# Twenty instead of eight shared groups ahead of the experts, with all late sends among them

## What is computed

```python
h = table[x]                                   # embedding
h = h + attention(layernorm(h))                # 8 heads
x2 = layernorm(h)
shared = gelu(x2 @ Ws1 + bs1) @ Ws2 + bs2      # for every row, 128 -> 512 -> 128
y = shared + bank(x2, sp) + bank(x2, fq)       # two banks of 8 experts each
out = h + y
# bank: each row goes to its top-1 expert, which takes 1280 rows at most;
#       expert = gelu(rows @ W1 + b1) @ W2 + b2, times the gate
```

## Time and profile before

| | |
|---|---|
| median of 3 runs | 1516.28 us (1511.69 to 1517.81) |
| span of the profiled execution | 1551.0 us (the page gives this and no other time of it) |
| PE busy | 1486.1 us, 96% of the span |
| DVE, ACT, POOL busy | 1049.6, 1148.1, 969.7 us |
| mean granted TensorE clock | 0.990 |

### The profile page before, as it was taken

The page is one execution under the profiler, slowest core; times in us unless marked ns, Lnnn a source line. Parts: engine busy times, 40 slices in busy tenths (PEclk is TensorE's granted clock), DMA queues, the critical chain, the costliest instruction groups (busy, mean ns, idle before and its releaser), DMA issues. The chain is left out here.

```text
span 1551.0 us, 33789 instructions
## 1 busy us (share of the span) xinstructions
PE 1486.1 (96%) x11128; PEld 1370.1 (88%) x11128; DVE 1049.6 (68%) x2810; ACT 1148.1 (74%) x3470; POOL 969.7 (63%) x998
## 2 busy tenths in 40 slices
PE   6789999999999999999999999978889999999999
PEld 3479999999999999999999999877888999999999
DVE  7977787788788788778788787642333343346666
ACT  6788888888888888888888888844444555556655
POOL 7575568887887887887887886643566566520000
PEclk9999999999999999999999999989999999999999
DMA  7224412112111111111111110112333323456665
GB/s 261 114 74 160 145 40 68 48 48 59 38 40 58 37 35 56 34 34 48 43 34 37 54 34 26 58 45 56 75 94 83 85 72 87 120 153 190 184 191 146
DMA packets 171503, 126.48 MB, mean 82 GB/s; under 512 B 30309, under 2 KB 154959, under 8 KB 171330
## 3 DMA queue, kind: packets, MB, share of 16 engines
q1 hardware_dynamic: 153794, 104.15, 22.7%
q0 software_dynamic: 17536, 20.17, 4.7%
HBM read 61.64 MB, written 78.66 MB: 90 GB/s over the span
## 5 line engine op out<-in xcount | busy, mean ns | idle before, releaser
L1138 ACT ACTIVATE expd<-masked,nmax 128x128 f32<-128x128 f32 x1024 | 395.9, 393 | 0.2 <-DVE nmax L1286 0.2
L938 POOL TENSOR_TENSOR prob<-expd,rtotal 128x1024 f32<-128x1024 f32 x128 | 243.2, 1900 | 126.8 <-DVE rtotal L1255 121.3
L1275 DVE COPY_PREDICATED masked<-off_diag,ps_s 128x1024 f32<-128x1024 int32 x128 | 174.7, 1365 | 143.5 <-PE ps_s L1031 143.5
L1071 PE MATMUL ps_o<-u,probT 128*128 128x128 f32 x2048 | 249.1, 275 | 0.0
L1071 PEld LDWEIGHTS ps_o<-u,probT 128*128 128x128 f32 x2048 | 239.0, 191 | 0.0
L1138 ACT ACTIVATION_READ_ACCUMULATOR expd<-masked,nmax 128x1 f32 x1024 | 196.6, 192 | 0.0
L1147 ACT ACTIVATE u<-ps_ut 128x1024 f32<-128x1024 f32 x128 | 131.4, 1026 | 66.5 <-PE ps_ut L1082 55.2
L1162 ACT ACTIVATE probT<-ps_ut 128x1024 f32<-128x1024 f32 x128 | 131.5, 1027 | 45.5 <-PE ps_ut L1039 37.9
L1231 DVE TENSOR_TENSOR w_lo<-ps_w,w_hi 128x512 fp32r<-128x512 f32 x256 | 164.4, 681 | 0.9 <-ACT w_hi L1171 0.9
L1171 ACT ACTIVATE w_hi<-ps_w 128x512 fp32r<-128x512 f32 x256 | 146.2, 596 | 15.9 <-PE ps_w L1057 9.3
L1286 DVE TENSOR_REDUCE nmax<-masked 128x8 f32<-128x1024 f32 x128 | 155.6, 1216 | 2.4
(11 more groups left out here) (252 smaller groups left out, 3914.8 us busy)
## 6 DMA issues: line engine op xcount, KB each, us to landing
turned<-x2T SPq DMA_DIRECT2D x32, 256.0 KB
answers_sp<-zeros SPq DMA_DIRECT2D x16, 512.0 KB
answers_fq<-zeros SPq DMA_DIRECT2D x16, 512.0 KB
xT<-turned SPq DMA_DIRECT2D x56, 128.0 KB
sh_back<-answers_sp SPq DMA_DIRECT2D x56, 128.0 KB, 2.3
sh_back<-answers_fq SPq DMA_DIRECT2D x56, 128.0 KB, 2.5
out<-res SPq DMA_DIRECT2D x56, 128.0 KB, 2.1
h_sb<-in_L_tok_weight SPq DMA_DIRECT2D x12, 512.0 KB, 6.2
```

The lines of the kernel that those rows point to most:

```text
L938: nc.gpsimd.tensor_tensor(prob[k % 2][:, :].rearrange("p (g j) -> p g j", g=H), expd[k % 2][:, :].rearrange("p (g j) -> p g j", g=H), rtot ...
L1071: mm = nc.tensor.matmul(ps_o[:, 0:D], probT[k % 2][:, g * N:(g + 1) * N], u[k % 2][:, g * D:(g + 1) * D], start=(g == 0), stop=(g == H - 1))
L1138: ins = nc.scalar.activation(expd[(k - 1) % 2][:, g * N:(g + 1) * N], masked[(k - 1) % 2][:, g * N:(g + 1) * N], ACT.Exp, bias=nmax[(k - 1 ...
L1275: nc.vector.copy_predicated(masked[k % 2][:, :].rearrange("p (g j) -> p g j", g=H), off_diag[:, :].unsqueeze(1).to_broadcast([P, H, N]), p ...
```

## The change

HEAD goes from 8 to 20, so 20 groups run ahead of the experts and 44 in the last stage; the tables of stages are filled to match, with stage 4 at k = 135, 5 at 136, 6 at 138 and the rest at 139. All 32 sends of the last 16 tiles, both banks, move behind POOL's other work of `attention`, into `late_sends`: one after every U (semaphore `head_up`) and one after every T (`head_turned`) from stage 2 to stage 18. `experts` holds no send any more. SP waits for every send before it loads the experts' first rows. In the last stage the head's rows are summed as 20 groups of 256 beside every second step from step 1, with four sums a group, two in step k and two in step k + 1.

```diff
-HEAD = 8
+HEAD = 20
-        AFTER = {129: (0,), 130: (1,), 131: (2,), 132: (3,), 136: (4,), 138: (5,), 139: range(6, HEAD + 2)}
-        BEHIND = {129: (0,), 130: (1,), 131: (2,), 134: (3,), 137: (4,), 139: range(5, HEAD + 2)}
+        AFTER = {129: (0,), 130: (1,), 131: (2,), 132: (3,), 135: (4,), 136: (5,), 138: (6,), 139: range(7, HEAD + 2)}
+        BEHIND = {129: (0,), 130: (1,), 131: (2,), 134: (3,), 135: (4,), 137: (5,), 139: range(6, HEAD + 2)}
+        SENDS_FROM = HEAD - 2 - (TILES - LATE)
...
-                sp.wait_ge(s_sent[k], TILES // 16 * 64 - 32)
+                sp.wait_ge(s_sent[k], TILES // 16 * 64)
...
-                    need_apart(pool, S["routed"], batch(i, t) + 1)
-                    late = isinstance(i, int) and tile(i, t) >= LATE
-                    for b in range(1 if late else BANKS):
-                        send(nc, sent, x2, to_row, t, b, s_sent[t // 2 % 8])
+                    if t < LATE:
+                        pool.wait_ge(S["routed"], batch(i, t) + 1)
+                        for b in range(BANKS):
+                            send(nc, sent, x2, to_row, t, b, s_sent[t // 2 % 8])
+            def late_sends():
+                for n in range((TILES - LATE) * BANKS):
+                    q, b, e = n // BATCH // BANKS, n // BATCH % BANKS, n % BATCH
+                    t = LATE + q * BATCH + e
+                    if e == 0:
+                        pool.wait_ge(S["routed"], t // BATCH + 1)
+                    if n % 2 == 0:
+                        pool.wait_ge(S["head_up"], n // 2 + SENDS_FROM)
+                    else:
+                        pool.wait_ge(S["head_turned"], n // 2 + SENDS_FROM + 2)
+                    send(nc, sent, x2, to_row, t, b, s_sent[t // 2 % 8])
             pipelined(pool, step, BODY, FIRST, LAST, LEAD, END, link, PCHAIN)
+            late_sends()
...
-                    if isinstance(i, int) and group(i, a) == GROUPS:
-                        sp.wait_ge(S["late"], 16 * LATES)
...
-                if isinstance(i, int) and k in LATE_AT:
-                    send(nc, sent, x2, to_row, LATE + LATE_AT.index(k), 1, S["late"])
...
-        HEADS_FROM = 4
-        def head_tile(i, k):
-            n = (k - HEADS_FROM) // 3
-            return (n, n) if (k - HEADS_FROM) % 3 == 0 and 0 <= n < 2 * HEAD else None
+        HEADS_FROM = 1
+        def head_group(k):
+            n = (k - HEADS_FROM) // 2
+            return n if (k - HEADS_FROM) % 2 == 0 and 0 <= n < HEAD else None
...
+                n = head_group(k + 2)
+                if n is not None:
                     need(sp, S["one_out"], n - 1)
                     for b in range(BANKS):
-                        sp.dma_start(one_back[b][n % 2][:, :], answers[b][bass.ds(t * P, P), :]).then_inc(s_one[n % 2], 16)
+                        sp.dma_start(one_back[b][n % 2][:, :, :], head_rows(answers[b], n)).then_inc(s_one[n % 2], 16)
...
+                n = head_group(k - 2)
+                if n is not None:
                     need(sp, S["one_out"], n + 1)
-                    sp.dma_start(out[bass.ds(t * P, P), :], one_out[n % 2][:, :]).then_inc(s_one_put[n % 2], 16)
+                    sp.dma_start(head_rows(out, n), one_out[n % 2][:, :, :]).then_inc(s_one_put[n % 2], 16)
...
+                n = head_group(k)
+                if n is not None:
                     dve.wait_ge(s_one[n % 2], (n // 2 + 1) * 32)
+                    need(dve, S["one_out"], n)
+                    for b in range(2):
+                        t = 2 * n + b
+                        ins = nc.vector.scalar_tensor_tensor(one_part[:, b, :], one_back[0][n % 2][:, b, :], gates[:, 2 * t:2 * t + 1],
+                                                             h_sb[:, t * D:(t + 1) * D], ALU.mult, ALU.add)
+                    ins.then_inc(S["one_part"], 1)
+                n = head_group(k - 1)
+                if n is not None:
+                    dve.wait_ge(S["one_part"], n + 1)
                     need(dve, s_one_put[n % 2], n // 2 * 16)
+                    for b in range(2):
+                        t = 2 * n + b
+                        ins = nc.vector.scalar_tensor_tensor(one_out[n % 2][:, b, :], one_back[1][n % 2][:, b, :], gates[:, 2 * t + 1:2 * t + 2],
+                                                             one_part[:, b, :], ALU.mult, ALU.add)
+                    ins.then_inc(S["one_out"], 1)
```

More of the change, by code:

```diff
@@ L978, in step @@
                         pool.wait_ge(s_zeroed, 16 * BANKS * FILLS)
-                    need_apart(pool, S["routed"], batch(i, t) + 1)
-                    late = isinstance(i, int) and tile(i, t) >= LATE
-                    for b in range(1 if late else BANKS):
-                        send(nc, sent, x2, to_row, t, b, s_sent[t // 2 % 8])
+                    if t < LATE:
[13 more added lines that the diff above has]
+                    send(nc, sent, x2, to_row, t, b, s_sent[t // 2 % 8])
             pipelined(pool, step, BODY, FIRST, LAST, LEAD, END, link, PCHAIN)
+            late_sends()
             for k in range(8):
-                pool.wait_ge(s_sent[k], TILES // 16 * 64 - 32)
+                pool.wait_ge(s_sent[k], TILES // 16 * 64)
         @block.tensor
@@ L1475, in experts @@
     LOADS = 64
-    LATES = TILES - LATE
-    LATE_AT = tuple(range(1, 1 + 2 * LATES, 2))
     with ExitStack() as s:
@@ L1492, in experts @@
         ps_o = [s.enter_context(nc.psum_tensor(f"ex_ps_o{k}", [P, 512], F32)) for k in range(2)]
-        S = {n: sem(n) for n in ("turned", "xhi", "xlo", "up", "gelu", "down", "out", "late", "next_hi")}
+        S = {n: sem(n) for n in ("turned", "xhi", "xlo", "up", "gelu", "down", "out", "next_hi")}
         S["w_hi"], S["w_lo"] = first.s_hi, first.s_lo
@@ L1681, in shared_ffn @@
         part = [sb(f"part{k}", [P, 2, D]) for k in range(2)]
-        one_back = [[sb(f"one_back{b}_{k}", [P, D]) for k in range(2)] for b in range(BANKS)]
-        one_part, one_out = sb("one_part", [P, D]), [sb(f"one_out{k}", [P, D]) for k in range(2)]
+        one_back = [[sb(f"one_back{b}_{k}", [P, 2, D]) for k in range(2)] for b in range(BANKS)]
+        one_part, one_out = sb("one_part", [P, 2, D]), [sb(f"one_out{k}", [P, 2, D]) for k in range(2)]
         ps_h = [s.enter_context(nc.psum_tensor(f"sh_ps_h{k}", [P, FC, G], F32)) for k in range(2)]
@@ L1704, in dram_rows, with head_rows @@
             return t[bass.ds((group(i, k) + HEAD) * G, G), :].rearrange("(s p) d -> p s d", p=P)
-        HEADS_FROM = 4
-        def head_tile(i, k):
-            n = (k - HEADS_FROM) // 3
-            return (n, n) if (k - HEADS_FROM) % 3 == 0 and 0 <= n < 2 * HEAD else None
+        HEADS_FROM = 1
+        def head_group(k):
+            n = (k - HEADS_FROM) // 2
+            return n if (k - HEADS_FROM) % 2 == 0 and 0 <= n < HEAD else None
+        def head_rows(t, n):
+            return t[bass.ds(n * G, G), :].rearrange("(s p) d -> p s d", p=P)
         @block.sync
@@ L1727, in step @@
                         sp.wait_ge(s_scattered[r], 32 * ALL // RING)
-                if head_tile(i, k):
-                    t, n = head_tile(i, k)
+                n = head_group(k + 2)
+                if n is not None:
                     need(sp, S["one_out"], n - 1)
                     for b in range(BANKS):
-                        sp.dma_start(one_back[b][n % 2][:, :], answers[b][bass.ds(t * P, P), :]).then_inc(s_one[n % 2], 16)
+                        sp.dma_start(one_back[b][n % 2][:, :, :], head_rows(answers[b], n)).then_inc(s_one[n % 2], 16)
                 a = k + 2
@@ L1742, in step @@
                     sp.dma_start(dram_rows(out, i, k - 1), res[(k - 1) % 2][:, :, :]).then_inc(s_put[(k - 1) % 2], 16)
-                if head_tile(i, k - 3):
-                    t, n = head_tile(i, k - 3)
+                n = head_group(k - 2)
+                if n is not None:
                     need(sp, S["one_out"], n + 1)
-                    sp.dma_start(out[bass.ds(t * P, P), :], one_out[n % 2][:, :]).then_inc(s_one_put[n % 2], 16)
+                    sp.dma_start(head_rows(out, n), one_out[n % 2][:, :, :]).then_inc(s_one_put[n % 2], 16)
             pipelined(sp, step, BODY, FIRST, LAST, 4, GROUPS + 2)
@@ L1751, in _ @@
             for k in range(2):
-                sp.wait_ge(s_one_put[k], 16 * HEAD)
+                sp.wait_ge(s_one_put[k], 16 * len(range(k, HEAD, 2)))
         @block.tensor
@@ L1826, in step @@
                                             ALU.add).then_inc(S["out"], 1)
-                if head_tile(i, k - 2):
-                    t, n = head_tile(i, k - 2)
+                n = head_group(k)
+                if n is not None:
                     dve.wait_ge(s_one[n % 2], (n // 2 + 1) * 32)
-                    need(dve, s_one_put[n % 2], n // 2 * 16)
[L1832 to L1837, removed]
+                    need(dve, S["one_out"], n)
[7 more added lines that the diff above has]
+                    dve.wait_ge(S["one_part"], n + 1)
```

(3 more changed lines are left out.)

## The result

| | before | after |
|---|---|---|
| median of 20 runs each, same chip | 1514.24 us (1511.42 to 1519.19) | 1517.67 us (1514.25 to 1522.19) |
| ratio after to before | | 1.002, interval 1.0012 to 1.0028 |
| span of the profiled execution | 1551.0, a second profile 1511.9 | 1516.9 |
| mean granted TensorE clock in it | 0.990, in the second 0.997 | 0.996 |

The change costs 3.4 us, 0.2%: less than the 0.5% that the prediction takes as the bound, though the interval excludes a ratio of 1. The first profile of before, the one whose rows stand ahead of the prediction, is of an execution that lasted longer than any timed one: its span alone is 32 us above the slowest of the 20.

The account below looks back on a forecast made before the run. PE's pace was taken as the bound wherever no pause stands. Terms 3.6 - 1 + 0.7 = +3.3 us, less 1 for pauses, gave 1516.3 + 2.3, about 1519 us; range 1499 to 1527.

Parts of the forecast that it names:

- No pauses in the timed runs: Late signals idling PE in head and experts, seen in the profile, take only 0 to 10 us of timed runs.
- Rivals A and C: A: timed runs hold the pauses too, 1486 or 1508, chance 0.24; C: pauses follow sends into head, about 1530, chance 0.03.
- The size of the pauses: In the first profile, 16.2 us in the head and 17.6 in the experts, taken as 30 to 34 us.
- The sum of +3.3 us: Costs of the longer head, drain and last stage's start together: 3.6 - 1 + 0.7, before 1 us off for pauses.
- Twelve groups, +3.6: Twelve groups moved into the head, each stage 3.46 us with transposes against 3.16 in the last stage: +3.6 us.
- The drain, -1: Stage 4 in step 135 gives PE work between the last x2 transposes and the logits, where it waited: -1 us.
- The sends, 0: 32 sends spaced over head stages stay under PE, and POOL's relief in the experts is off the path: 0 us.
- The last stage: PE stays the bound at 3.16 us a step, two sums fitting in DVE's slack of 0.57; start costs +0.7 us.
- Rival B: The last stage leaves PE's pace once a step loses over 0.57 us of slack; 1532 to 1545 us, chance 0.12.

Follow-up runs that it names:

- f1: The kernel before, unchanged, profiled a second time; 1513.62 us in one run.
- e4: The kernel before with its 16 late fq sends in steps 1 to 16 of the experts, one in each; 1517.6 us, ratio 1.0025.
- f2: The changed kernel with its twenty head groups' turned rows loaded from DRAM, without transposes and normalisation there; 1516.59 us, ratio 1.0016 to before.
- e1: The changed kernel with its 16 late fq sends put back into the experts, one every second step; 1517.08 us, ratio 1.0023 to before.
- e2: The changed kernel with its late sends unspaced, without the waits for head_up and head_turned; 1518.14 us, ratio 1.003 to before.
- f4: The kernel before with the change's table of stages alone, eight groups; 1517.45 us, ratio 1.0025.
- g1: f2 with a second PSUM buffer for the up-products of the groups ahead of the experts; 1511.74 us, ratio 0.997 to before.
- g2: g1 with late sends unspaced and the head groups' sums begun three steps later in the last stage; 1511.45 us, ratio 0.9974 to before.

## Why the prediction came out right, step by step

- **No pauses in the timed runs: right.** The reason that I gave for them, POOL without gaps, fell: the same sends make none in `f1`, and denser ones in `e4` make another wait. One execution had them, and none of the 20 timed runs of before is above 1519.19 us; what raised its signals late stays open, since it did not come back. Rivals A and C lose their ground with it.
- **The size of the pauses was too small.** I put them at 30 to 34 us; the two profiles of before differ by 39.1. Counted as in the table, 14.4 of that lie ahead of the experts (I had 16.2), 22.1 in them (I had 17.6) and 0.6 in the last stage; the other 2 stand before the count starts. So the profile's span was forecast at 1524 and is 1516.9. The sum of +3.3 us is what was measured (+3.4). That the point of 1519 us lies only 1.3 us from the median is partly luck: it starts from 1516.28 us, 2 us above the median of the 20 runs, and takes off 1 us for pauses that these runs do not show.
- **Twelve groups, +3.6: right in size** (3.44 - 3.16 = 0.28 us each, 3.36), **half the cause.** "In the head a stage also has T" holds for PE: 0.22 of the 0.28 us are T, the rest is a slower U. What I did not see is the ring through one PSUM buffer, 3.41 us by itself: "That holds if ACT and DVE keep up" had 0.03 us to spare. The same reading made me expect 20 x 0.28 = 5.6 us from removing T; `f2` saved 1.1 us by its median, which the intervals do not tell from nothing.
- **The drain, -1: right in after** (-0.97 as the rest of a difference; the x2T wait of 0.7 us is gone), but only with the longer head. "Routing of the last batch comes up to one stage later, under twelve more stages" was the condition that carries it: with eight groups the same edit costs 3.3 us.
- **The sends, 0: right.** The intervals of `e1` and `e2` do not tell them from after; in their profiles it takes 65.03 us to the experts (65.04 in after) and 270.2 us through them.
- **The last stage: right.** PE keeps 3.16 us a step, DMA is at 0.82 (estimate 0.81). DVE waits 0.70 us for PE where 0.57 was expected:

```profile
1420.51 0.43 DVE L1836 TENSOR_TENSOR res<-sh_ps_o,sh_part 128x256 f32<-128x256 f32 x1 [0.70 <-PE sh_ps_o L1786]
1420.85 0.61 DVE L1854 SCALAR_TENSOR_TENSOR sh_one_out<-sh_one_back,gates,sh_one_part 128x128 f32<-128x128 f32 x2
...
1423.67 0.42 DVE L1836 TENSOR_TENSOR res<-sh_ps_o,sh_part 128x256 f32<-128x256 f32 x1 [0.70 <-PE sh_ps_o L1786]
```

  Rival B fell: its condition, a step that loses its slack, is not met. The start costs 0.57 us by the difference against +0.7, which profiles of one and the same last stage do not tell from nothing.

## What to carry to other kernels

That the passes on the busiest engine add up to a loop's period does not show that removing one of them shortens it: look also for a buffer that one engine fills and another empties, and see whether start of fill, end of emptying and the next start close the same period. Here both did, at 3.44 and 3.41 us: removing T gave 0.03 us a stage, removing T and giving a second buffer 0.22. An edit that fills a hole ahead of a router or any producer delays all that hangs on it, so ask what starts the next stage before counting the hole as gain. And where a profiled span and the timed median lie far apart, profile the unchanged kernel once more before explaining the difference.

## What was not expected of the hardware

- One execution of an unchanged program held 11 late signals worth 47.1 us of DVE's waits, and 20 more in other waits of DVE and ACT; a second profile of it and the twelve profiles of changed kernels held none.
- The same twelve matmuls of an up pass take 1.46 us in the last stage of after, 1.52 us in the head, and 1.50 us in the last stage of `e1`, whose steps are 3.20 us throughout instead of 3.16; no row names a wait for it.
- Behind an idle time of 3.3 us in `f4` the experts' first passes took 1.5 us more, at a granted clock of 0.50. But `g1` and `e4` fell to 0.55 and 0.63 in the same place, behind idle times of 0.85 and 0.79 us in `g1`, 0.86 and 0.69 in `e4`; like ones (0.85 and 0.78 in after) left the clock at 1.00 in after, `f2` and `g2`. What decides between these stays open.
